# KDA stage of an eight-stage network kernel: scores placed beside the lower product, masks ahead of additions, first tap ahead of the residuals, and the query's inverse norm folded into the output norm

## The reference, cut to what matters

```python
q = _conv_silu(x @ Wq, conv_q).reshape(b, t, H, DH)
k = _conv_silu(x @ Wk, conv_k).reshape(b, t, H, DH)
v = _conv_silu(x @ Wv, conv_v).reshape(b, t, H, DH)
g = -jnp.exp(A_log)[None, None, :, None] * _softplus_stable(g_raw)
beta = jax.nn.sigmoid(x @ Wb)
qf = _l2norm(q) * DH ** (-0.5)          # t * rsqrt(sum(t*t) + 1e-6)
kf = _l2norm(k)
def step(state, inp):
    q_i, k_i, v_i, g_i, b_i = inp
    state = state * jnp.exp(g_i)[..., None]
    inner = jnp.einsum('bhk,bhkv->bhv', k_i, state)
    state = state + jnp.einsum('bhk,bhv->bhkv', b_i[..., None] * k_i, v_i - inner)
    o_i = jnp.einsum('bhk,bhkv->bhv', q_i, state)
    return (state, o_i)
rstd = jax.lax.rsqrt(jnp.mean(o * o, axis=-1, keepdims=True) + EPS)
o = o * rstd * norm_w * jax.nn.sigmoid(g_out)
return o.reshape(b, t, KD) @ Wo
```

## Time and profile before

| | us |
|---|---|
| median of 3 runs | 6265.92 |
| lowest and highest run | 6243.98, 6275.91 |
| the profiled execution | 6272.03 |
| its span | 6270.3 |
| the KDA passes in it | from about 2180 to about 4360 |
| busy over the span: PE, DVE, ACT, POOL | 5487.5, 3220.0, 2789.8, 2304.6 |

### The profile page before, as it was taken

The page is one execution under the profiler, slowest core; times in us unless marked ns, Lnnn a source line. Parts: engine busy times, 40 slices in busy tenths (PEclk is TensorE's granted clock), DMA queues, the critical chain, the costliest instruction groups (busy, mean ns, idle before and its releaser), DMA issues. The chain is left out here.

```text
span 6270.3 us, 125078 instructions
## 1 busy us (share of the span) xinstructions
PE 5487.5 (88%) x53008; PEld 3632.2 (58%) x53008; DVE 3220.0 (51%) x4649; ACT 2789.8 (44%) x5107; POOL 2304.6 (37%) x1583
## 2 busy tenths in 40 slices
PE   6888699755999599989989989998999988889999
PEld 5777466543666266666666666665444456664444
DVE  5555444434444376776776677675212166552221
ACT  3233444454444456555655655665211166662111
POOL 4554100001000176777777677675222200002222
PEclk8999799877999799999999999999999988889999
DMA  0000100000000000000000000000211100002111
GB/s 29 3 2 2 33 1 1 16 0 33 1 1 3 22 17 23 18 17 23 18 17 17 24 17 17 23 18 9 107 40 40 34 11 0 0 1 108 39 40 46
DMA packets 60618, 137.02 MB, mean 22 GB/s; under 512 B 11638, under 2 KB 24054, under 8 KB 58842
## 3 DMA queue, kind: packets, MB, share of 16 engines
q1 hardware_dynamic: 60122, 129.79, 6.2%
HBM read 127.26 MB, written 2.50 MB: 21 GB/s over the span
## 5 line engine op out<-in xcount | busy, mean ns | idle before, releaser
L607 PE MATMUL ps<-moe_xn_all,moe_w 128*128 128x512 f32 x1792 | 810.5, 595 | 0.0
L720 DVE TENSOR_TENSOR moe_h<-moe_silu,ps 128x512 f32<-128x512 f32 x224 | 153.9, 687 | 936.2 <-ACT moe_silu L662 929.1
L607 PEld LDWEIGHTS ps<-moe_xn_all,moe_w 128*128 128x128 f32 x1792 | 341.2, 191 | 424.1 <-issue 423.5
L662 ACT ACTIVATE moe_silu<-ps 128x512 f32<-128x512 f32 x224 | 133.8, 597 | 986.5 <-PE ps L607 986.4
L1797 DVE SCALAR_TENSOR_TENSOR kda_cv<-kda_pre,kda_w_front,kda_cv 128x1024 f32<-128x1024 f32 x297 | 554.8, 1885 | 1.3
L563 POOL TENSOR_TENSOR moe_h<-moe_h,moe_cb 128x512 f32<-128x512 f32 x176 | 233.6, 1327 | 696.4 <-DVE moe_h L720 696.4
L1983 POOL TENSOR_TENSOR kda_g<-kda_g,kda_f 128x512 f32<-128x512 f32 x225 | 395.4, 1757 | 205.7 <-DVE kda_rows L1975 197.1
L617 PE MATMUL ps<-moe_h,moe_w 128*128 128x512 f32 x896 | 420.4, 592 | 0.0
L1681 PE MATMUL ps<-kda_xn_all,kda_w_front 128*128 128x512 f32 x808 | 373.6, 606 | 26.0 <-DMA kda_w_front<-in_Kw 23.5
L1975 POOL TENSOR_TENSOR kda_rows<-kda_q,kda_f 128x512 f32<-128x512 f32 x225 | 361.1, 1605 | 16.6 <-POOL kda_f L1984 1.6
L1984 POOL TENSOR_TENSOR kda_f<-kda_f 128x512 f32<-128x512 f32 x225 | 313.9, 1395 | 17.6
(11 more groups left out here) (505 smaller groups left out, 12513.3 us busy)
## 6 DMA issues: line engine op xcount, KB each, us to landing
kda_col<-kda_beta SPq DMA_DIRECT2D x34, 512.0 KB, 3.9
moe_w<-in_Mw SPq DMA_DIRECT2D x6, 2816.0 KB, 19.6
moe_cb<-kda_beta SPq DMA_DIRECT2D x64, 256.0 KB, 3.1
kda_w_front<-in_Kw SPq DMA_DIRECT2D x34, 455.0 KB, 4.7
moe_cb<-kda_beta SPq DMA_DIRECT2D x32, 224.0 KB, 2.9
kda_w_out<-in_Kw SPq DMA_DIRECT2D x32, 192.5 KB, 2.4
moe_cb<-kda_beta SPq DMA_DIRECT2D x32, 192.0 KB, 2.8
moe_cb<-kda_beta SPq DMA_DIRECT2D x32, 160.0 KB, 2.7
```

The lines of the kernel that those rows point to most:

```text
L607: last = nc.tensor.matmul(ps_gu[u % 2][r], w13[:, k, i, r], n.xn[:, k, cols(c)], start=k == 0, stop=k == KD - 1)
```

## The change

1. On PE the scores of level l+1 are issued directly behind the lower product of level l, and the product `t_times_x` follows them; the small products of the tail and the projection stand behind it.
2. On DVE the masks and the a rows of the next level move ahead of `update` of the present level, and the taps move later. One tap of q (`first_tap`) moves from the start of the next pass to ahead of the two residual additions. `a_row` moves ahead of `scale`.
3. The query is no longer normalised: its sum of squares (PE), logarithm and root (ACT) and `q_row` (DVE) go. Instead ACT writes the query's squares into a buffer kept for two passes (`q_square`), and DVE adds them with a factor to the squares of y (`with_query`) ahead of the sum over the channels. The epsilon in the tail's logarithm changes (`eps[:, 4:5]`).
4. On POOL the columns' decays are widened before the wait for DVE's a rows, and the q rows of level 0 are scaled between the two widenings.
5. On ACT the last x copy stands behind the SiLU of v, the copy of the transposed values behind the logarithms.
6. The tile t2 and a separate lt6 go (lt6 lies in z), two q_sq tiles come; an unused mask of 128 x 448 is no longer loaded.

```diff
-            def squares(i):
+            def squares():
+                pe.wait_ge(m.proj_read, at(m.proj_read, 2))
+                pe.wait_ge(m.sq_ready, at(m.sq_ready, 1))
...
+            def q_square():
+                act.wait_ge(m.silu_ready, at(m.silu_ready, 1))
+                if in_chain:
+                    act.wait_ge(m.ysum_ready, at(m.ysum_ready, 1))
+                nc.scalar.activation(o.q_sq[:], o.q[:], ACT.Square).then_inc(m.qsq_ready, 1)
...
+            def first_tap():
+                dve.wait_ge(m.head_read, at(m.head_read, 2))
+                tap_dve(step, m.conv_ready, 0, 0, w)
...
-            def q_row():
...
+            def with_query():
+                dve.wait_ge(n.ysq, at(n.ysq, 2))
+                if turn.index:
+                    dve.wait_ge(m.qsq_ready, at(m.qsq_ready, -1))
+                nc.vector.scalar_tensor_tensor(y_sq[:], o.q_sq[:], QUERY_EPS * KDA_HEAD, y_sq[:], ALU.mult,
+                                               ALU.add).then_inc(m.ysum_ready, 1)
...
+            scale_rows(nc.gpsimd, o, 0, 0, n.first_scaled)
             pool.wait_ge(n.g_clear, at(n.g_clear, 1))
+            widen_columns(step, o, 0)
+            pool.wait_ge(m.silu_ready, at(m.silu_ready, 3))
+            scale_rows(nc.gpsimd, o, 0, 1, n.first_scaled)
             pool.wait_ge(n.first_scaled, at(n.first_scaled, 2))
-            widen(step, o, 0)
+            widen_rows(step, o, 0)
...
                 pool.wait_ge(n.scaled, at(n.scaled, 2 * l))
+                widen_columns(step, cur, l)
                 pool.wait_ge(n.rows_scaled, at(n.rows_scaled, l))
-                widen(step, cur, l)
+                widen_rows(step, cur, l)
```

The new order of PE from level 4 on (before it was `lt_times_t`, a small product, `t_times_x`, a front product, `scores`):

```diff
+            lt_times_t(4)
+            scores(5)
+            t_times_x(4)
+            tail.y_of(1)
+            f.squares()
+            lt_times_t(5)
+            last_scores()
+            t_times_x(5)
+            f.values()
+            tail.square_sums()
+            last_x()
+            pe.wait_ge(m.vt_in_sb, at(m.vt_in_sb, 1))
```

On ACT the copy for `t_times_x(5)` now stands behind the SiLU of v:

```diff
+            copy_x(4)
             tail.square(1)
             f.silu(2)
-            copy_x(4)
-            act.wait_ge(n.e1_in_sb, at(n.e1_in_sb, 1))
-            f.values()
-            f.log_sum(0)
+            copy_x(5)
+            f.log_sum()
             f.log_decay()
-            copy_x(5)
-            f.log_sum(1)
-            tail.log()
+            f.q_square()
```

More of the change, by code:

```diff
@@ L1847, in column @@
                                                ALU.mult).then_inc(m.rows_ready, 1)
-            return Calls(clip=clip, tap=tap, corr=corr, q_row=q_row, a_row=a_row, column=column)
+            return Calls(clip=clip, tap=tap, corr=corr, a_row=a_row, column=column)
         def tail_pe(pe, o, w, quad):
@@ L1933, in log @@
                 act.wait_ge(n.yss_ready, at(n.yss_ready, 1))
[L1934 removed]
+                nc.scalar.activation(y_sq[:], two(TAIL), ACT.Ln, scale=1.0 / KDA_HEAD, bias=g.eps[:, 4:5]
                                      ).then_inc(n.ylog, 1)
@@ L1968, in residual @@
                 nc.vector.tensor_tensor(xs, two(OUT[k]), xs, ALU.add).then_inc(n.x_done, 1)
-            return Calls(inner=inner, right_side=right_side, gate=gate, scale=scale, residual=residual)
+            return Calls(inner=inner, right_side=right_side, gate=gate, with_query=with_query, scale=scale,
+                         residual=residual)
         def scale_rows(engine, o, l, r, done):
@@ L2261, in chain_dve @@
             tail.inner(0)
+            a_rows(2)
+            masks(1)
             f.clip()
[L2263 to L2265 removed]
+            masks(2)
             f.tap(0, 2)
[L2267 removed]
             dve.wait_ge(n.t_ready, at(n.t_ready, 3))
             update(1)
+            a_rows(3)
             tail.gate(0)
+            f.tap(1, 0)
             f.tap(1, 1)
[L2272 to L2275 removed]
+            masks(3)
+            a_rows(4)
             update(2)
             tail.right_side()
[L2278 to L2283 removed]
+            f.tap(1, 2)
             masks(4)
             a_rows(5)
[L2286 to L2288 removed]
+            update(3)
+            tail.inner(1)
+            f.tap(2, 0)
             masks(5)
             a_rows(6)
+            update(4)
+            f.corr(0)
+            f.tap(2, 1)
+            f.tap(2, 2)
+            tail.with_query()
+            tail.gate(1)
+            last_masks()
             update(5)
[L2292 removed]
             f.corr(1)
             f.corr(2)
+            f.a_row()
             tail.scale()
[L2296 to L2297 removed]
             f.column()
+            first_tap()
             tail.residual(0)
```

195 lines of the change are left out of this document (78 added, 117 removed).

## The result

| | before | changed |
|---|---|---|
| median, us | 6269.41 (4 runs) | 6184.89 (4 runs) |
| lowest and highest | 6243.98, 6275.91 | 6178.79, 6190.20 |
| profiled execution, span | 6272.03, 6270.3 | 6190.20, 6188.4 |

The ratio is 0.9872, with a 95% interval of 0.9842 to 0.9902: 1.3% faster. The forecast was 6190 in a range of 6080 to 6260.

A forecast was written before the change was run, and what follows sets the result against it. PE's work and late mask waits set the old pass; the POOL and DVE queue came next. 51.8 + 13.25 + 0.75 = 65.8 us a pass, 2.4 less over 32 passes, plus 2 us outside, gave 6190, range 6080 to 6260.

The forecast's parts named there:

- S to the end of the widening of level 5: From S, POOL's first operation on the rows, through its level 5 widening: 42.6 us as one POOL and DVE queue.
- from there to T: From POOL's level 5 widening through DVE's taps, SiLU and x copy to T, PE's further product of level 5: 9.2 us.
- T to S at the full clock: From PE's further product of level 5 to POOL's next first rows operation, along ACT's chain: 13.25 us, before 15.56.
- the clock's charge a pass: PE running at the lower clock after its wait: 1.51 us in every second pass, 0.75 a pass.
- PE's work a pass at the full clock: PE's busy time falls from 60.95 to 59.0 us as one sum of squares goes.
- PE's wait ahead of T: New PE stall before the further product of level 5, for ACT's x copy behind the SiLU: 2 to 3 us.
- the same count: POOL and DVE operations added as one queue over POOL's stretch: 45.2 us for the kernel before, against 46.2 measured.
- the clock eats it: Rival, chance 0.20: PE's stall lowers the clock, 1.5 us more in every pass; pass 67.5 us, time 6248.
- The outer bounds: Limits of a pass from POOL's stretch, the taps ahead of the SiLU and the clock: 62.7 to 70.3 us.
- at nothing: First tap ahead of the residuals delays the first residual and PE's gate product about 2 us, claimed to cost nothing.
- PE stays the bound: Rival, chance 0.15: POOL and DVE fit their turns better, only PE's chain remains; pass 61.5 us, time 6055.
- Slower: Rival, chance 0.08: POOL's stretch stays at 46.2 with two last taps behind it; pass 69.4 us, time 6310.

The follow-up runs named there:

- experiment 7: Changed kernel with the key's sum of squares issued twice on PE (1.92 us more work a pass): 6154.66 us, ratio 0.9818.
- experiment 1: Kernel before with only the fold of the query's norm (part 3 of the change), every engine in its old order: 6184.33 us, ratio 0.9862.
- experiment 4: Changed kernel with the first correction behind level 5's update, the last x copy ahead of v's SiLU, and query's squares ending ACT's pass: 6048.58 us, ratio 0.9641.
- Experiments 5 and 6: Second tap of v left out in the passes: 5 in the changed kernel, 6075.55 us (0.9691); 6 in the kernel before, 6273.82 us (1.0004).
- experiment 2: Changed kernel with the first correction moved from ahead of v's two last taps to behind the update of level 5: 6081.32 us, ratio 0.9698.
- Experiment 9: Changed kernel with POOL's widening of columns in levels 1 to 6 again behind the wait for DVE's a rows: 6180.64 us, ratio 0.9875.
- experiment 8: Changed kernel with the first tap of q moved back behind the residual additions: 6199.25 us, ratio 0.9882.
- experiment 11: Experiment 4's kernel with the key's sum of squares issued twice on PE: 6107.28 us, ratio 0.9749.
- experiments 3: Changed kernel with ACT's last x copy moved ahead of the SiLU of v: 6165.44 us, ratio 0.9837.

## Why the prediction was right, and where it was right by luck

| step | forecast | measured |
|---|---|---|
| S to the end of the widening of level 5 | 42.6 | 42.61 |
| from there to T | 9.2 | 8.76 |
| T to S at the full clock | 13.25 | 12.98 (experiment 7) |
| the clock's charge a pass | 0.75 | 1.55 |
| pass | 65.8 | 65.92 |
| PE's work a pass at the full clock | 59.0 | 59.0 in the old order (experiment 1), 58.4 in experiment 4's |
| PE's wait ahead of T | 2 to 3 | 2.07 |
| waits for masks, us in the stage | under 60 | 24.1 |

**The mechanism held.** PE's stall did move from the masks to the copy behind the SiLU of v, and the new path ran over the queue of POOL and DVE and then over ACT, with every stretch within 0.5 us. Experiments 5 and 6 show the change of bound, and 2 and 5 the size of a turn, 2.0 us where the count had 2.2. That POOL's stretch came out to within 0.01 us is luck: the same count had missed 1.0 in the kernel before, and it misses 1.6 in experiment 1 (45.2 against 46.8).

**The mis-sized term is the clock.** I charged 1.51 us in every second pass, as the earlier trace rows showed before. The stall moved, and its successor of 2.07 us is followed by a fall in every pass. It costs time because the sum for y then ends late (6.4 us behind T where I had 5.4), and ACT waits for it. The line that sums y shows it: shortest, median and longest ns of one product in the changed kernel,

```profile
L1912 PE MATMUL ps<-kda_y_sq,net_ones_w x132: 592/966/1062, 2204.4 to 4292.5; 128*128 128x512 f32 x132
```

where experiment 4 has 592 as its median. Half of the rival "the clock eats it" was true: every pass pays about 1.5. The Trainium skill, "TensorE: Matmul & The Clock Gate", section "HAM oscillation — how this bites in real kernels", whose rule gave 66.6 a pass, was right in kind: the wait returns each round and so does the lower clock. The waits of the page's example are longer, some 3 to 5 us; here a wait of 2.07 us was enough, and the measurement decides. The measured 65.92 is under the 66.6 only because the rest of the pass was shorter than forecast. Without the clock I had 51.8 + 13.25 = 65.05; experiment 7 gives 64.37. An error of +0.7 there (0.4 ahead of T, 0.3 behind it) and one of -0.8 in the clock cancelled. That the forecast of the pass is within 0.1 is luck too. The outer bounds are added up wrongly: from the terms named they are 65.8 - 1.0 - 2.2 - 0.75 = 61.9 and 65.8 + 3.6 + 1.1 + 0.75 = 71.3 and not 62.7 and 70.3. The forecast does not hang on them.

**Two reasons were wrong or unproved.** The missed 1.0 us of the count, I wrote, came "from waits that the earlier widening of columns now fills". Experiment 9 refutes that: without the early widening the stretch is the same. POOL's waits for a rows are gone in the new order of DVE all the same; that it is the a rows ahead of the update that removed them is argued from the order and was not run by itself. And I cost the late residual and gate "at nothing". It is so for T (experiment 8 moves it by 0.2 only), but PE does wait 1.4 us there, and what it saves elsewhere shows only through the clock.

**The rivals.** "PE stays the bound" fell: 1.92 us more work for it cost nothing (experiment 7). It becomes true once the stall ahead of T is gone (experiment 11). "Slower" rested on POOL's stretch staying at 46.2; it does stay there in the old order (46.8 in experiment 1), and the new order takes it to 42.6.

**What the prediction didn't ask** is what each part brings. It took the gain as one sum over a new path. The fold alone brings all of it, and the re-ordering shortens the path at full clock by only 0.8 more (65.18 to 64.37: 1.3 less up to T, 0.5 more behind it) and pays about that back in clock, on the medians all of it. Which of the moves pays and which costs was not split. What the new order could give, 136 us more than measured, lay behind three operations that stood at the wrong place in their queues: a correction and the query's squares too early, a copy too late. Of these, the correction alone gives 104; the copy alone 19; the share of the square was not run by itself.

## What to carry to other kernels

Where two engines take turns, count their operations as one queue and look at which of them stand in front of the operand that the next bound engine waits for: one that isn't needed yet costs a whole pair of turns (2.0 us here, 32 times). When a change moves a stall, price the new stall twice, once as time and once as clock, and look into the new place of it before you reuse the old rate. When a large change of order goes together with a small saving of work, run the saving by itself.

## What the runs showed of the hardware

- More work can be faster: 1.92 us of products added to PE in each pass, inside a wait of 2.07 us, took 30 us off the launch (6184.89 to 6154.66). In 20 of 31 passes the granted clock then stayed at 1.00, the 2.4 GHz level (L1706 1.06 us instead of 1.94), where it had fallen in every pass.
- Waits of up to 1.7 us for the gate (experiment 2) were followed by no fall over the whole stage, clock 1.00 from 2180 to 4171 us; a wait of 1.96 to 2.08 us was followed by one in every pass (changed kernel, experiments 3 and 8), and one of 1.93 to 1.95 us in about every second pass of the kernel before. The length of the wait alone does not decide: experiment 7 and experiment 1, whose longest waits in the stage are 1.7 and 1.8 us, still have falls, in 11 and 7 of 31 passes.
- A turn is priced by who meets whom: the last two taps of v beside POOL take 4.28 us together, 2.14 each, where an operation of this size that meets nothing takes 1.22, and over the stage DVE's busy time grows although the taps are as many as before.
